# A five-stage FFN loop with matmuls grouped by type and a DMA transpose, in a fused attention and quantised-FFN kernel on Trainium2

## The reference

```python
base = einsum('btd,od->bto', x, W)                     # 1024 -> 1024
logits = einsum('btd,ed->bte', x, Wr) + bias           # 8 experts
topw, topi = top_k(logits, 2); weights = softmax(topw)
gates = sum(one_hot(topi, 8) * weights)
h = einsum('btd,erd->bter', x, A)                      # 8 experts x rank 16 = 128 numbers
z = base + 2.0 * einsum('bter,bte,eor->bto', h, gates, B)
# quantised feed-forward of z in bfloat16, q = clip(round(zs / scale), -127, 127), scale = max|zs| / 127 of a token
qg, sg = dynamic_quant(z, inv_gate); qu, su = dynamic_quant(z, inv_up)
inter = silu((qg @ w_gate.T) * sg * s_wgate) * ((qu @ w_up.T) * su * s_wup)     # 1024 -> 512
inter = clip(inter, -10, 10).astype(bfloat16)
qi, si = dynamic_quant(inter, inv_inter)
out = x + (qi @ w_down.T) * si * s_wdown               # 512 -> 1024
```

## Time and profile before

| | us |
|---|---|
| median of 3 runs | 2319.82 (2318.79 to 2320.93) |
| the profiled execution's own time | 2318.84 |
| its span, first to last instruction | 2317.2 |
| FFN stage, from PE's first matmul of `z` | 1595.7 to the end |
| iterations t = 3 to 31 of the FFN loop | 1631.15 to 2259.40 |
| iteration t = 32 up to the end of the last `z` | 2259.40 to 2277.40 |
| from there to the end | 2277.40 to 2317.2 |

### The profile page before, as it was taken

One profiled execution on the slowest core, in us unless ns is written; L12 is line 12 of the kernel. 1 busy time (PEld: TensorE's weight loads), 2 busy tenths in 40 slices (PEclk: granted clock), 3 DMA queues, 4 the chain that ended last, 5 costly groups with the idle time before them and its releaser, 6 DMA issues.

```text
span 2317.2 us, 47569 instructions
## 1 busy us (share of the span) xinstructions
PE 2213.8 (96%) x19328; PEld 1797.9 (78%) x19360; DVE 1403.4 (61%) x2392; ACT 732.2 (32%) x1182; POOL 1387.7 (60%) x1135
## 2 busy tenths in 40 slices
PE   6999999999999999999998999999999999999995
PEld 5888877888877888788887788887777777777774
DVE  5354564445555545654546965666777777777775
ACT  4222242222242222422224321213334334334332
POOL 6887877877778787787875800001545545545543
PEclk9999999999999999999999999999999999999998
DMA  4112122111131111211125255467111111111111
GB/s 143 59 59 71 51 83 92 56 65 56 61 103 68 65 51 64 84 58 63 51 67 182 97 188 182 155 177 210 37 37 54 54 36 54 54 36 54 54 36 46
DMA packets 121004, 186.32 MB, mean 80 GB/s; under 512 B 15490, under 2 KB 52482, under 8 KB 120322
## 3 DMA queue, kind: packets, MB, share of 16 engines
q1 hardware_dynamic: 117970, 180.61, 23.9%
q0 software_dynamic: 2864, 3.28, 0.8%
HBM read 136.66 MB, written 50.33 MB: 81 GB/s over the span
## 4 chain that ended last, share of the span: by engine, by line
PE 67%; DVE 13%; POOL 7%; issue 6%; ACT 4%; SPq 2%; DMA 1%; POOLq 0%; DVEq 0%; ACTq 0%
PE acc L699 33%; PE acc L1095 6%; PE att L1095 6%; PE acc L1510 4%; PE att L730 3%; PE att L1571 2%; PE att L1582 2%; POOL f_raw L1280 2%; DVE f_gap L1450 2%; PE att L739 2%; PE att L754 2%; DVE prob L539 2%; PE acc L1595 2%; POOL f_silu L1286 2%; POOL f_silu L1283 2%
## 5 line engine op out<-in xcount | busy, mean ns | idle before, releaser
L699 PE MATMUL acc<-y_hi,w_slot_hi 128*128 128x512 f32 x1344 | 541.9, 403 | 26.0 <-issue 7.6
L699 PE MATMUL acc<-y_lo,w_slot_hi 128*128 128x512 f32 x1344 | 528.2, 393 | 0.0
L699 PE MATMUL acc<-y_hi,w_slot_lo 128*128 128x512 f32 x1344 | 527.9, 393 | 0.0
L345 POOL TENSOR_TENSOR w_slot_lo<-w_raw,w_slot_hi 128x512 fp32r<-128x512 f32 x329 | 423.6, 1288 | 26.3
L699 PEld LDWEIGHTS acc<-y_hi,w_slot_hi 128*128 128x128 f32 x1344 | 254.7, 190 | 86.2 <-issue 30.6
L343 POOL CAST w_slot_hi<-w_raw 128x512 fp32r<-128x512 f32 x329 | 218.1, 663 | 157.5 <-PE acc L699 131.7
L699 PEld LDWEIGHTS acc<-y_hi,w_slot_lo 128*128 128x128 f32 x1344 | 255.0, 190 | 54.8
L699 PEld LDWEIGHTS acc<-y_lo,w_slot_hi 128*128 128x128 f32 x1344 | 255.1, 190 | 48.5
L348 POOL TENSOR_TENSOR w_raw<-w_raw 128x512 f32<-128x512 f32 x188 | 259.8, 1382 | 29.1 <-DMA w_raw<-wu 25.2
L546 DVE COPY cx<-att 128x512 f32<-128x512 f32 x63 | 43.6, 691 | 306.4 <-PE att L754 277.2
L1293 POOL TENSOR_TENSOR f_raw<-f_raw,f_x_all 128x1024 f32<-128x1024 f32 x32 | 76.1, 2379 | 251.8 <-DVE f_raw L1497 251.8
(11 more groups left out here) (177 smaller groups left out, 4074.8 us busy)
## 6 DMA issues: line engine op xcount, KB each, us to landing
w_raw<-wu SPq DMA_DIRECT2D x192, 256.0 KB, 3.1
...
context_T<-cx SPq DMA_DIRECT2D x63, 256.0 KB, 3.5
...
x_T<-xa SPq DMA_DIRECT2D x48, 256.0 KB, 2.1
```

The lines of the kernel that those rows point to most:

```text
L345: pool.tensor_tensor(w_lo[:, k], raw, w_hi[:, k].bitcast(F32), ALU.subtract).then_inc(w_set, 1)
L699: ins = pe.matmul(bank, w[:, k, c, :], v[:, k, c, :], start=(k in (0, 1, 5) and c == 0 and i == 0), stop=(c == C // 2 - 1 and i == 2), ski ...
```

## The change

The loop gets a fifth stage, `has(4)`, so 36 iterations. Output scaling (`si`, `o1`, `o2`, `fin`, the store) moves from stage 3 to stage 4. PE's order becomes three groups: full float32 (`h` of tile t, `ht` of t-1, `si` of t-4), fp32r (48 + 6 matmuls of `z` of tile t-1 in one piece), bf16 (`qi` transposes of t-3, gate and up of t-2, down of t-3). The 16 PE transposes of `qb` go; SP issues two DMA transposes per tile from `qb[i]` into `qT[i]` in place of them, and DVE clips `qT[i]` in place. The banks `q_ps` that this frees become `d_ps`, in which the down product and the `qi` transposes now go. ACT copies `zb` of tile t-1 at the end of iteration t and not of tile t-2 at the start. DVE's queue is reordered to suit. `x_sb` has two buffers; the x that `fin` adds is loaded a second time, into `xr`, 512 KB more for each tile. SP's queue is written out without a loop. The core of the diff:

```diff
     x_all = at("x_all", [P, 4, C, P], F32, X_AT)
-    x_sb = [x_all[:, i] for i in range(4)]
-    b_raw = x_all[:, 3].rearrange("p c n -> p (c n)")
+    x_sb = [x_all[:, i] for i in range(2)]
+    xr = [x_all[:, 2 + i] for i in range(2)]
+    b_raw = xr[1].rearrange("p c n -> p (c n)")
...
     z_ps, g_ps = banks[0][:, 0:2], banks[1][:, 0:2]
-    q_ps = banks[0][:, 2:4].bitcast(BF16).rearrange("p i (c n) -> p i c n", n=P)
+    d_ps = banks[0][:, 2:4]
...
-    qi_ps = g_ps[:, 0, 0:INTER // 2].bitcast(BF16).rearrange("p (c n) -> p c n", n=P)
...
+    qi_ps = d_ps[:, 0, 0:INTER // 2].bitcast(BF16).rearrange("p (c n) -> p c n", n=P)
...
-        for j in range(3):
+        for j in range(UNROLL):
             body(TILES + j, j, lambda k, j=j: k > j)
...
-        def body(t, j, has):
-            if has(3):
-                sp.wait_ge(fin_set, t - 2)
-                if not (isinstance(t, int) and t == 3):
-                    sp.wait_ge(o_out, t * 16 - 48)
-                sp.dma_start(out[bass.ds(t - 3, 1)].rearrange("o p n -> (o p) n"),
-                             o_sb[(j + 1) % 2].rearrange("p c n -> p (c n)")).then_inc(o_out, 16)
-
-            if has(0) and not (isinstance(t, int) and t == 0):
-                if isinstance(t, int) and t == 2:
+        for t in range(TILES + 4):
+            if 1 <= t < TILES - 1:
+                sp.wait_ge(a_mm, t)
+                sp.wait_ge(xl_set, t)
+                load(sp, x_sb[(t + 1) % 2], t + 1, x_in[(t + 1) % 2])
+            if 3 <= t < TILES + 3:
+                if t == 4:
                     sp.wait_ge(b_lo_set, 1)
-                load_x(sp, (t + 1) % TILES, (j + 1) % 4)
-
-        tile_loop(sp, body)
-        sp.wait_ge(o_out, 16 * TILES)
-        sp.wait_ge(x_in[0], 16 * (TILES // 4 + 1))
+                elif t > 4:
+                    sp.wait_ge(fin_set, t - 4)
+                load(sp, xr[(t - 3) % 2], t - 3, xr_in[(t - 3) % 2])
+            if 2 <= t < TILES + 2:
+                if t > 2:
+                    sp.wait_ge(gu_mm, t * 2 - 4)
+                for i in range(2):
+                    sp.wait_ge(qb_set, t * 2 - 3 + i)
+                    sp.dma_start_transpose(qT[i][:], qb[i][:]).then_inc(turned[i], 16)
+            if t >= 4:
+                sp.wait_ge(fin_set, t - 3)
+                sp.dma_start(out[t - 4], o_sb[t % 2].rearrange("p c n -> p (c n)")).then_inc(o_out[t % 2], 16)
+        for i in range(2):
...
-            if has(3):
-                pool.wait_ge(o2_set, t - 2)
-                pool.tensor_tensor(o_sb[(j + 1) % 2], o_sb[(j + 1) % 2], x_sb[(j + 1) % 4], ALU.add)\
-                    .then_inc(fin_set, 1)
+            if has(4):
+                pool.wait_ge(xr_in[j % 2], pair_count(t - 4, j))
+                pool.wait_ge(o2_set, t - 3)
+                pool.tensor_tensor(o_sb[j % 2], o_sb[j % 2], xr[j % 2], ALU.add).then_inc(fin_set, 1)
...
         def body(t, j, has):
-            if has(2):
-                if isinstance(t, int) and t == 2:
-                    outputs_stored(act)
-                act.wait_ge(xg_set, t - 2)
-                act.wait_ge(xu_set, t - 2)
-                for b in range(2):
-                    act.wait_ge(z_mm, t * 2 - 3 + b)
-                    act.activation(zb[:, b * HALF:(b + 1) * HALF], z_ps[:, b], ACT.Copy).then_inc(zb_set, 1)
...
                     act.activation(xs[i], xs[i], ACT.Copy, bias=ROUND, scale=rinv[:, i:i + 1]).then_inc(rnd_set, 1)
-                    if i == 0 and not (isinstance(t, int) and t == 2):
-                        act.wait_ge(tq_mm, t * 2 - 4)
+                    if not (isinstance(t, int) and t == 2):
+                        act.wait_ge(turned[i], t * 16 - 32)
                     act.wait_ge(rnd_set, t * 2 - 3 + i)
                     act.activation(qb[i][:], xs[i], ACT.Copy, bias=-ROUND).then_inc(qb_set, 1)
...
                 act.activation(qi[:], xi[:], ACT.Copy, bias=-ROUND).then_inc(qi_set, 1)
+            if has(1):
+                if isinstance(t, int) and t == 1:
+                    outputs_stored(act)
+                act.wait_ge(xg_set, t - 1)
+                act.wait_ge(xu_set, t - 1)
+                for b in range(2):
+                    act.wait_ge(z_mm, t * 2 - 1 + b)
+                    act.activation(zb[:, b * HALF:(b + 1) * HALF], z_ps[:, b], ACT.Copy).then_inc(zb_set, 1)
+            if has(3):
                 act.wait_ge(ti_mm, t - 2)
                 act.wait_ge(d_mm, t - 3)
...
-            if has(3):
-                dve.wait_ge(gu_mm, t * 2 - 5)
-                dve.wait_ge(p1_set, t - 3)
-                dve.scalar_tensor_tensor(gt[:], g_ps[:, 0], sc[:, three, 0:1], sg_all[:], ALU.mult, ALU.mult)\
-                    .then_inc(gt_set, 1)
...
             if has(3):
+                dve.wait_ge(gu_mm, t * 2 - 5)
+                dve.wait_ge(p1_set, t - 3)
+                dve.scalar_tensor_tensor(gt[:], g_ps[:, 0], sc[:, three, 0:1], sg_all[:], ALU.mult, ALU.mult)\
+                    .then_inc(gt_set, 1)
+            if has(2):
+                dve.wait_ge(xg_set, t - 1)
+                row_max(0, xs[0], amax_set)
+                scale(0, two, amax_set, sc_set, rinv_set, t * 2 - 3)
...
+            if has(0):
+                dve.wait_ge(a_mm, t + 1)
+                dve.tensor_tensor(lg[:], s_ps[:, ER:NX], lang_bias[:, bass.ds(t, 1)].rearrange("p o e -> p (o e)"),
+                                  ALU.add).then_inc(lg_set, 1)
...
-            if has(2):
-                dve.wait_ge(gu_mm, t * 2 - 4)
-                for i in range(2):
-                    dve.wait_ge(tq_mm, t * 2 - 3 + i)
-                    dve.tensor_scalar(qT[i][:], q_ps[:, i], QMAX, -QMAX, ALU.min, ALU.max).then_inc(qT_set, 1)
+            if has(4):
+                dve.wait_ge(si_mm, t - 3)
             if has(1):
                 dve.wait_ge(ht_mm, t)
                 dve.wait_ge(z_mm, t * 2 - 2)
                 dve.tensor_copy(hg_hi[:], ht_ps).then_inc(hh_set, 1)
                 dve.wait_ge(hh_set, t)
                 dve.tensor_tensor(hg_lo[:], ht_ps, hg_hi[:].bitcast(F32), ALU.subtract).then_inc(hl_set, 1)
+            if has(4):
+                o = o_sb[j % 2]
+                dve.tensor_copy(si_sb[:], si_ps).then_inc(si_set, 1)
+                dve.wait_ge(si_set, t - 3)
+                dve.wait_ge(d_mm, t - 3)
+                if not (isinstance(t, int) and t < 6):
+                    dve.wait_ge(o_out[j % 2], pair_count(t - 6, j))
+                dve.tensor_tensor(o, d_ps.rearrange("p b (c n) -> p (b c) n", n=P),
+                                  si_sb[:].unsqueeze(1).broadcast_to([P, C, P]), ALU.mult).then_inc(o1_set, 1)
+                dve.wait_ge(o1_set, t - 3)
+                dve.tensor_tensor(o, o, sd_c[:].unsqueeze(2).broadcast_to([P, C, P]), ALU.mult).then_inc(o2_set, 1)
+            if has(2):
+                for i in range(2):
+                    dve.wait_ge(turned[i], t * 16 - 16)
+                    dve.tensor_scalar(qT[i][:], qT[i][:], QMAX, -QMAX, ALU.min, ALU.max).then_inc(qT_set, 1)
...
+            if has(0):
+                if isinstance(t, int) and t == 0:
+                    pe.wait_ge(ar_in, 32)
+                pe.wait_ge(x_in[j % 2], pair_count(t, j))
+                pe.wait_ge(hc_set, t)
+                for c in range(C):
+                    ins = pe.matmul(h_ps, x_sb[j % 2][:, c, :], ar_w[:, c, :], start=(c == 0), stop=(c == C - 1))
+                ins.then_inc(a_mm, 1)
+            if has(1):
+                pe.wait_ge(hg_set, t)
+                if not first:
+                    pe.wait_ge(hl_set, t - 1)
+                if has(4) and not (isinstance(t, int) and t == 4):
+                    pe.wait_ge(si_set, t - 4)
+                pe.transpose(ht_ps, hg[:], ident[:]).then_inc(ht_mm, 1)
+            if has(4):
+                pe.wait_ge(diag_set, t - 3)
+                if not has(1):
+                    pe.wait_ge(hl_set, TILES)
+                    pe.wait_ge(si_set, t - 4)
+                pe.matmul(si_ps, ones[:], diag[:], start=True, stop=True).then_inc(si_mm, 1)
             if has(1):
                 pe.wait_ge(xl_set, t)
                 if first:
                     pe.wait_ge(link.x2_set, PRODUCTS)
-                else:
-                    pe.wait_ge(zb_set, t * 2 - 3)
-                linear(one, 0, range(C), first)
-            if has(0):
-
...
+                for b in range(2):
+                    if not first:
+                        pe.wait_ge(zb_set, t * 2 - 3 + b)
                     for c in range(C):
-                        ins = pe.transpose(q_ps[:, i, c], qb[i][:, c * P:(c + 1) * P], ident_b[:])
-                    ins.then_inc(tq_mm, 1)
-            if has(1):
-                linear(one, 1, range(2, 4), first)
...
-            if has(3):
-                pe.wait_ge(ut_set, t - 2)
-                pe.wait_ge(qi_set, t - 2)
-                for c in range(CI):
-                    ins = pe.transpose(qi_ps[:, c], qi[:, c * P:(c + 1) * P], ident_b[:])
```

(108 more changed lines are left out.)

66 lines of the change are left out of this document (22 added, 44 removed), and 2 rows, old and new, of tables (qi_ps, x_in).

## The result

The changed kernel takes 2269.59 us, median of 4 runs (2266.86 to 2272.32), against 2319.31 (2316.59 to 2320.93) for the kernel before on the same chip: ratio 0.9781, 95% interval 0.9767 to 0.9795. Forecast were 2272.5 us and a range of 2260 to 2302. The profiled execution's own time is 2266.86 us, its span 2265.2.

The account below looks back on a forecast made before the run. PE was taken as the bound, before and after, at 20.14 us an iteration for 21.68. 2317.2 - 44.7 + 3.6 - 5.3 = 2270.8 for the span, plus 1.64 gave 2272.5 us, range 2260 to 2302.

Parts of the forecast that it names:

- start, to t = 3: First iterations: PE idles before `h` of tile 1, which runs at half clock ahead of z of tile 0; +3.6 us.
- 29 periods: Iterations t = 3 to 31: each goes from 21.68 to 20.14 us, 44.7 us less in all.
- t = 32: Iteration of the last z: only `ht`, `si` and z stand ahead, 12.7 us for 18.0, so -5.3.
- drain: Chain from the last z to the program's end, 39.8 us before: taken as unchanged, -4 to +5.
- The 16 transposes: PE's transposes of `qb` leave each iteration: 0.88 us less.
- The wait for `qi`: PE's idle time ahead of the `qi` transposes, for ACT, goes: 0.26 us less an iteration.
- The wait of gate for `o1`: PE's wait ahead of gate, taken away by `d_ps`: counted as nothing, being covered but for a product's start.
- The types: PE returns to fp32r once an iteration, not six times: 5 x 0.08 = 0.40 us less, bounds 0 and 0.55.
- The forecast's own groups: PE's three groups in the new order: float32 2.1 us, z 12.4, bf16 5.4.
- Rival C: Types weren't the cost; only PE's transposes and wait go: period 20.54, 2284 us, chance 0.10.
- Rival B: DVE becomes the bound, held by POOL's instructions: 2284 to 2304 us, at the middle 2294; chance 0.15.
- Rival D's ring: DVE's queue waits for late DMA transposes lasting T: period 8.4 + T, saving gone at T = 13.3 us; chance 0.12.

Follow-up runs that it names:

- e2: Sixteen bf16 matmuls of zeros put in five places between z's fp32r matmuls of the changed kernel; 2312.68 us, period 21.45.

## Why the prediction was right

The parts, against the forecast's, in us of the span (before 2317.2, after 2265.2, -52.0):

| part | forecast | measured |
|---|---|---|
| ahead of the stage | 0 | -2.1 (first `h` 1592.36, then 1590.24; scatter) |
| start, to t = 3 | +3.6 | +3.2 (1632.22 - 1631.15, and the 2.1) |
| 29 periods | -44.7 | -48.4 (29 x 1.67) |
| t = 32 | -5.3 | -5.4 |
| drain | 0 | +0.7 |

The -2.1 is luck: nothing ahead of the stage was changed, and in the second profile of the changed kernel the first `h` starts at 1593.01. The forecast's mechanism (PE bound, transposes and changes of type taken from it, DVE and the DMA transposes hidden) is what the profile shows. Its saving of 1.54 us a period came near the measured 1.68 in part because errors in single terms went opposite ways.

- *The period.* 20.00 us, not 20.14. These rows take the 1.68 us apart: two of PE's waits before (us, times, longest), then one iteration before (PE, DVE, and what PE's weight loads waited for, counted over 16 iterations), then PE after.

```profile
PE att L1555 <- ACT f_qi L1347: 7.2, 28, 0.3
PE att L1582 <- issue: 4.8, 28, 0.2
```

```profile
2032.32 0.27 PE L1550 MATMUL att<-ident,f_hg 128*128 128x128 f32 x1
...
2037.73 0.40 PE L1510 MATMUL acc<-f_w_hi,f_x_lo 128*128 128x512 f32 x1
2038.30 1.67 PE L1582 MATMUL att<-f_gu_w,f_qT 128*128 128x512 bf16 x7 [0.17 <-issue]
...
2036.79 1.23 DVE L1494 TENSOR_TENSOR f_raw<-att,f_si_sb 128x1024 f32<-128x1024 f32 x1 [1.46 <-PE att L1571]
...
PEld att L1582 <- DVE f_raw L1494: 6.0, 16, 0.4
```

```profile
2033.96 0.27 PE L1525 MATMUL att<-ident,f_hg 128*128 128x128 f32 x1
2034.07 0.39 PE L1531 MATMUL att<-f_diag,f_ones 128*128 128x128 f32 x2
2034.21 0.47 PE L1543 MATMUL acc<-f_w_hi,f_x_hi 128*128 128x512 f32 x1
```

  - The 16 transposes: 0.88, as forecast.
  - The wait for `qi`: 0.42, not 0.26. From `ht` to the `qi` transposes there were 2032.85 - 2032.32 = 0.53 us, and from `ht` to what follows it there are now 0.11. Beside the idle time shown, the end of `ht` lay bare, which otherwise runs under the next matmul.
  - The wait of gate for `o1`: 0.12, forecast as nothing ("its cover was complete but for the start of a product"). The 4.8 us of the list are not that wait. In the 29 iterations has 4060 matmuls and 4088 weight loads: 28 records of a matmul are missing, and gate shows 7 of 8. Its matmuls are 0.216 apart (16 in 3.62 us after the change, 0.38 for the last), so the one without a record began at 2038.08, when `o1` (L1494) was over at 2038.02. Without a wait it would have been 2037.73 + 0.23 = 2037.96.
  - The types: what is left, 1.68 - 0.88 - 0.42 - 0.12 = 0.26, forecast 0.40. The forecast took all returns at 0.08 us. Behind short bf16 matmuls that holds, with 0.03 more in the matmuls behind it (e2). Behind the 128 x 512 matmuls of gate and up it is 0.02: from the first of up at 2041.21 to the second fp32r matmul behind it at 2043.18 are 1.97 us, and 8 x 0.216 + 0.228 = 1.96. And the new order has a price of its own: `h` takes 1.91 us behind the down product (2032.05 to 2033.96) where it took 1.76 behind `z`.

  So 0.28 us were missing in two waits, and 0.14 too many stood in the types. The forecast's own groups would have shown a gap: 2.1 + 12.4 + 5.4 = 19.9 us, 0.24 under its 20.14; measured they are 2.16 + 12.36 + 5.48 = 20.00. Rival C (types cost nothing) falls with e2.
- *DVE.* Forecast 18.9 of 20.1, measured 18.5 of 20.0, and DVE is held where it was said: `gap` free, `xi`'s scaling + 1.15, the clips + 2.1.
- *Rival B* was given 0.15 as a bound through what it calls POOL's lock: a DVE instruction held to the end of POOL's, as `gap` was (1.75 us for 0.16). It isn't what the changed kernel does, but it lies near: DVE late by 0.37 us, or a tie lost by 0.05. It isn't a sum of instructions that grows, as the forecast had it ("at least 0.3 in DVE's queue"), but a second state of the same loop, 1.4 us longer at once.
- *DMA transposes.* Forecast 3 to 4 us, measured 3.0; 4.4 us to spare, forecast "some 4". Rival D's ring holds with 7.3 + T for 8.4 + T.
- *Start.* As forecast, once the 2.1 us ahead of the stage are taken off. `h` of tile 1 begins 8.43 us behind the first `h` (1598.67 - 1590.24), forecast 8.24, and runs 3.64 us, at a granted clock of 0.58 (1594 to 1600 us) and 0.69 (1600 to 1603). The half clock of the forecast is the 0.50 of the earlier trace rows, a stretch in which PE is busy 1.01 of 3.00 us; that it would hold for `h` too, as 2 x 1.76 = 3.5 us to `ht`, was the author's estimate, and it was 3.47 (1598.67 to 1602.14), against 1.91 in the loop at a clock of 1.00. `z` follows at 1602.17, which is 1604.3 in the times of the kernel before; forecast was 1604.4. +3.2 for +3.6.
- *What stays open.* What decides the tie of `xs[0]` and `xs[1]` in favour of one kernel or another (it isn't chance from run to run: the 12 executions with `qi` by DMA, alone and with the early `z`, all take 2298.43 to 2305.19 us, and the nine of the changed kernel 2266.86 to 2272.52), and what made DVE late in the loop's first iterations with the 16 matmuls at the end; and why the matmuls behind a return to fp32r are 0.230 us apart for a while and not 0.227.
